# Weight splits behind the exponentials, the keys' low part ahead of the routing, and other orders at the ends of two stages

## What is computed

```python
x = x + tanh(g_xattn[0]) * L0_xattn(layernorm(x), ctx)   # 16 heads of 64, causal, softmax
x = x + tanh(g_ffn[0])   * L0_ffn(layernorm(x))          # 8 experts + 4 zero experts, top 2
x = x + tanh(g_xattn[1]) * L1_xattn(layernorm(x), ctx)   # 16 heads of 8, softmax
x = x + tanh(g_ffn[1])   * L1_ffn(layernorm(x))          # 8 routed experts (top 2) + 2 shared
```

## Time and profile before

| | us |
|---|---|
| median of 3 runs | 267.52 |
| lowest, highest | 266.63, 267.69 |
| the profiled execution | 266.27 |
| its span, first to last instruction | 264.5 |
| busy: PE / DVE / ACT / POOL | 246.9 / 185.1 / 118.8 / 73.9 |
| mean granted clock of TensorE | 0.996 |

### The profile page before, as it was taken

The page is one execution under the profiler, slowest core; times in us unless marked ns, Lnnn a source line. Parts: engine busy times, 40 slices in busy tenths (PEclk is TensorE's granted clock), DMA queues, the critical chain, the costliest instruction groups (busy, mean ns, idle before and its releaser), DMA issues.

```text
span 264.5 us, 7195 instructions
## 1 busy us (share of the span) xinstructions
PE 246.9 (93%) x2917; PEld 207.7 (79%) x2917; DVE 185.1 (70%) x487; ACT 118.8 (45%) x207; POOL 73.9 (28%) x93
## 2 busy tenths in 40 slices
PE   8979999989999999988999999999689999999994
PEld 2557778978899888867999999888566888787783
DVE  1646788866563998899327588446785996887773
ACT  2565455555422455425124344654346767423210
POOL 2356384535531633341001023000210332201100
PEclk9999999999999999999999999999999999999998
DMA  6619600040000000059591000340000000000011
GB/s 192 205 45 267 201 4 4 2 121 1 2 2 0 4 2 2 0 196 297 183 377 38 0 2 0 119 161 1 2 0 2 2 5 2 4 1 2 0 40 40
DMA packets 13232, 16.75 MB, mean 63 GB/s; under 512 B 2064, under 2 KB 10640, under 8 KB 13072
## 3 DMA queue, kind: packets, MB, share of 16 engines
q1 hardware_dynamic: 13056, 16.03, 18.9%
q10 hardware_dynamic: 144, 0.26, 0.5%
HBM read 12.62 MB, written 3.67 MB: 62 GB/s over the span
## 4 chain that ended last, share of the span: by engine, by line
PE 75%; DVE 13%; POOL 4%; issue 4%; ACT 3%; DVEq 0%; POOLq 0%
PE OC L1238 11%; PE MB L1191 5%; PE MB L1081 5%; PE SP L1152 5%; PE OC L1174 5%; PE TP L1161 5%; PE MB L1082 4%; PE MB L1083 4%; PE SP L1088 3%; PE OC L1180 2%; PE SP L1081 2%; PE SP L1083 2%; PE SP L1082 2%; PE MB L1328 2%; PE TP L1376 2%
## 5 line engine op out<-in xcount | busy, mean ns | idle before, releaser
L415 POOL TENSOR_TENSOR S_sb<-S_sb,nmax 128x512 f32<-128x512 f32 x32 | 33.2, 1041 | 38.9 <-DVE nmax L767 38.9
L896 DVE SCALAR_TENSOR_TENSOR x_sb<-OC,gate,x_sb 128x128 f32<-128x128 f32 x64 | 18.0, 344 | 22.4 <-PE OC L1238 22.3
L1238 PEld LDWEIGHTS OC<-f_w,hid 128*128 128x128 f32 x256 | 30.9, 192 | 1.4
L758 DVE TENSOR_TENSOR S_sb<-SP,maskb 128x512 f32<-128x512 f32 x32 | 21.9, 685 | 14.1 <-PE SP L1152 13.9
L1238 PE MATMUL OC<-f_w,hid 128*128 128x128 f32 x256 | 31.4, 276 | 0.0
L767 DVE TENSOR_REDUCE nmax<-S_sb 128x4 f32<-128x512 f32 x32 | 22.0, 686 | 1.1
L539 ACT ACTIVATE PT<-TP 128x512 f32<-128x512 f32 x32 | 19.0, 593 | 7.2 <-PE TP L1161 7.1
L1161 PE MATMUL TP<-id_sb,S_sb 128*128 128x128 f32 x128 | 19.6, 275 | 1.9 <-POOL S_sb L415 1.8
L385 POOL TENSOR_SCALAR var_eps<-mv 128x4 f32<-128x4 f32 x8 | 2.0, 246 | 67.3 <-DVE mv L710 67.3
L523 ACT ACTIVATE arena_f<-MB 128x512 f32<-128x512 f32 x16 | 9.6, 599 | 23.8 <-PE MB L1083 23.3
L1174 PE MATMUL OC<-PT,arena_f 128*32 128x128 f32 x512 | 17.7, 275 | 2.7 <-issue 2.1
(11 more groups left out here) (218 smaller groups left out, 586.4 us busy)
## 6 DMA issues: line engine op xcount, KB each, us to landing
k_dram<-f_r SPq DMA_DIRECT2D x4, 512.0 KB, 9.2
arena_f<-in_zeros SPq DMA_DIRECT2D x1, 2048.0 KB, 9.6
arena_r<-k_dram SPq DMA_DIRECT2D x1, 2048.0 KB, 8.0
w_raw<-in_w SPq DMA_DIRECT2D x4, 384.0 KB, 4.1
ew_raw<-in_f0w SPq DMA_DIRECT2D x1, 1024.0 KB, 7.1
f_w<-in_f0w SPq DMA_DIRECT2D x1, 1024.0 KB, 10.6
arena_r<-q_dram SPq DMA_DIRECT2D x2, 512.0 KB, 4.4
ew_raw<-in_f1w SPq DMA_DIRECT2D x1, 640.0 KB, 10.8
```

What stands on the lines that cost most here:

```text
L415: g.tensor_tensor(S_sb[:, b], S_sb[:, b], nmax[:, b].unsqueeze(2).to_broadcast([P, H4, P]), ALU.add).then_inc(shifted, 1)
L758: v.tensor_tensor(S_sb[:, b].rearrange("p (r a) k -> p r a k", r=2), SP[:, :, 2 * P * b:2 * P * (b + 1)].rearrange("p r (a k) -> p r a k", ...
L896: ins = v.scalar_tensor_tensor(x_sb[:, b, :], OC[:, n % 2, batch(t)], gate0[:, b, e:e + 1], x_sb[:, b, :], ALU.mult, ALU.add)
L1238: ins = mm(OC[:, n % 2, batch(t)], hid[:, n % 2, c, batch(t)], f0_w2[:, e, c, :], start=(c == 0), stop=(c == 1))
```

## The change

- ACT: `split_w0(1,0)` and `split_w0(1,1)` go ahead of the first `queries0`, and in units 0 to 13 `exp0(u,1)` goes ahead of the unit's hooks. POOL: its halves of the splits go one unit later (`split_w0(2,*)` from unit 0 to 1, `split_w0(3,*)` from 2 to 3, `split_f0` from 6..9 to 7..10), `add_bias(0,0)` from 3 to 4 and `best_difference(0,0)` from 14 to 15.
- DVE: part 1 of `route_best(0,0)` goes from unit 14, where it stood ahead of `keys1`, to the head of unit 15's hooks.
- Second attention on PE: `spread_queries(2)` and `(3)` go ahead of `turned1(2,0)`, `maxima1(3)` between the two `turned1(2,*)`, `scores1(4,*)` ahead of `values_of(1)`; at b = 7 `output1(0,0)` goes ahead of `maxima1(7)` (in the ring too), and 3 clock-keeping matmuls stand where there were 5.
- Second expert stage: `spread_gates(4)` goes from turn 4 to turn 3, ahead of `logits(1,1)`; `gates_turn(1)` goes ahead of `hidden1(6)`, and ACT's `gates_hi(1)` from behind turn 6 to behind turn 5. In the last turn DVE makes both products in two halves of 256 tokens, and PE waits for the second half only ahead of its third token block.

```diff
@@ ring_order
-        uses += ([("m", 7), ("y1", 0, 0), ("y1", 0, 1), ("o", 5)] if b == 7 else
+        uses += ([("y1", 0, 0), ("m", 7), ("y1", 0, 1), ("o", 5)] if b == 7 else
...
-        if pair1(n) < C1 - 1:
+        if pair1(n) < C1 - 1 and n != 4:
             uses.append(("b", n))
-        uses += {2: [("t", 3, 1)], 3: [("l", 1, 1)], 5: [("g", 1)]}.get(n, [])
+        uses += {2: [("t", 3, 1)], 3: [("b", 4), ("l", 1, 1)], 5: [("g", 1)]}.get(n, [])
@@ gpsimd
-            hooks = {0: [lambda: split_w0(2, 0), lambda: split_w0(2, 1)],
-                     2: [lambda: rstd_of(0, 1), lambda: split_w0(3, 0), lambda: split_w0(3, 1)],
-                     3: [lambda: add_bias(0, 0)], 5: [lambda: add_bias(0, 1)],
-                     6: [lambda: split_f0(0)], 7: [lambda: split_f0(1)], 8: [lambda: split_f0(2)],
-                     9: [lambda: split_f0(3)], 10: [lambda: rstd_of(1, 0)], 14: [lambda: best_difference(0, 0)]}
+            hooks = {1: [lambda: split_w0(2, 0), lambda: split_w0(2, 1)], 2: [lambda: rstd_of(0, 1)],
+                     3: [lambda: split_w0(3, 0), lambda: split_w0(3, 1)],
+                     4: [lambda: add_bias(0, 0)], 5: [lambda: add_bias(0, 1)],
+                     7: [lambda: split_f0(0)], 8: [lambda: split_f0(1)], 9: [lambda: split_f0(2)],
+                     10: [lambda: rstd_of(1, 0), lambda: split_f0(3)], 15: [lambda: best_difference(0, 0)]}
@@ scalar
             values0(0, 0)
+            split_w0(1, 0)
+            split_w0(1, 1)
             queries0(0, 0)
             queries0(0, 1)
             values0(0, 1)
-            split_w0(1, 0)
-            split_w0(1, 1)
...
                         exp0(u, 0)
                         values0(s, 1)
+                    exp0(u, 1)
                 for hook in hooks.get(u, ()):
                     hook()
                 if s >= STEPS:
                     exp0(u, 0)
-                exp0(u, 1)
+                    exp0(u, 1)
...
-            hooks = {1: [lambda: gates_hi(0)], 3: [...], 6: [lambda: gates_hi(1)]}
+            hooks = {1: [lambda: gates_hi(0)], 3: [...], 5: [lambda: gates_hi(1)]}
@@ vector, hidden1
+                if n == N1 - 1:
+                    wait_full(dve, ("b", n))
+                    for w in range(2):
+                        tok = slice(2 * P * w, 2 * P * (w + 1))
+                        v.tensor_tensor(hid[:, n % 2, 1, tok], hid[:, n % 2, 0, tok], bank[:, 1, tok], ALU.mult).then_inc(up1, 1)
+                        dve.wait_ge(up1, 2 * n + 2 * w + 1)
+                        v.tensor_tensor(hid[:, n % 2, 1, tok], hid[:, n % 2, 1, tok], ring(("b", n))[:, tok], ALU.mult
+                                        ).then_inc(up1, 1)
+                    return
@@ vector, hooks of the first attention
-                     14: [lambda: route_best(0, 0, (1,)), lambda: keys1(0), lambda: keys1(1)],
-                     15: [lambda: values1(0), lambda: values1(1), lambda: route_gates(0, 0)]}
+                     14: [lambda: keys1(0), lambda: keys1(1)],
+                     15: [lambda: route_best(0, 0, (1,)), lambda: values1(0), lambda: values1(1), lambda: route_gates(0, 0)]}
@@ tensor, expert1
+                    if n == N1 - 1 and t == 1:
+                        pe.wait_ge(up1, 2 * N1 + 2)
@@ tensor, second attention
             spread_queries(1)
+            spread_queries(2)
+            spread_queries(3)
             turned1(2, 0)
-            spread_queries(2)
+            maxima1(3)
             turned1(2, 1)
-            spread_queries(3)
             for b in range(3, B):
                 if b == B - 1:
+                    output1(0, 0)
                     maxima1(b)
-                    output1(0, 0)
-                    keep_clock(area_for("t", b, 0)[:, 0, 0:256], 5)
+                    keep_clock(area_for("t", b, 0)[:, 0, 0:256], 3)
                     output1(0, 1)
...
                 if b == 3:
-                    maxima1(b)
-                values_of(b - 2)
-                if b > 3:
-                    maxima1(b)
-                scores1(b + 1, 0)
-                scores1(b + 1, 1)
+                    scores1(b + 1, 0)
+                    scores1(b + 1, 1)
+                    values_of(b - 2)
+                else:
+                    values_of(b - 2)
+                    maxima1(b)
+                    scores1(b + 1, 0)
+                    scores1(b + 1, 1)
@@ tensor, second expert stage
             for n in range(2, N1):
-                if pair1(n) < C1 - 1 and n < N1 - 1:
+                if n == 5:
+                    gates_turn(1)
+                if pair1(n) < C1 - 1 and n not in (4, N1 - 1):
                     spread_gates(n)
                 if n + 1 < N1:
                     hidden1(n + 1)
                 if n == 3:
+                    spread_gates(4)
                     logits(1, 1)
-                if n == 5:
-                    gates_turn(1)
```

More of the change, by code:

```diff
@@ L692, in _ @@
             copy_outputs(B - 1)
-            hooks = {1: [lambda: gates_hi(0)], 3: [lambda: xnT_flat_copy(1), lambda: xnT_hi_copy(3, 1)], 6: [lambda: gates_hi(1)]}
+            hooks = {1: [lambda: gates_hi(0)], 3: [lambda: xnT_flat_copy(1), lambda: xnT_hi_copy(3, 1)], 5: [lambda: gates_hi(1)]}
             for n in range(N1):
```

## The result

| | us |
|---|---|
| changed kernel: median of 5 runs, lowest, highest | 262.56, 262.40, 266.69 |
| kernel before, beside it: median of 5 runs | 267.52 |
| ratio changed / before, 95% interval | 0.984, 0.980 to 0.988 |
| profiled execution of the changed kernel, its span | 266.69, 264.9 |

The change makes the kernel 1.6% faster, 4.2 us by the ratio; 3.3 was forecast for it. Executions of both kernels fall into steps by TensorE's mean granted clock. Changed: 262.2 to 262.8 at 0.999 or more, 264.2 at 0.993 and 266.7 to 267.0 at 0.977 to 0.981. At full clock the medians are 266.3 and 262.5: **3.8 us**.

A forecast was written before the change was run, and what follows sets the result against it. PE's work bounds the kernel, busy 246.9 of 264.5 us, so only waits can be won. Terms 2.2 + 0.55 - 0.4 + 0.8 + 0.15 = 3.3 off median 267.52 give 264.2 us, range 262.4 to 266.2.

The forecast's parts named there:

- Units 0 and 1: First attention's start: waits for POOL's split and for an exponential go, the late shift keeps part; gain 1.0 us.
- Units 2 and 3: Exponential ahead of splits gives 0.5 us, freed shift 0.2; running gain 1.7, then 1.3 at unit 4 after DVE blocking.
- L717 beside POOL's splits: Unit 3: moved splits slow DVE's normalising, 1.10 us lost there; held by the first split alone, running gain 1.3.
- the upper value: Running gain 1.9 us at unit 4 if DVE's L717 loses nothing beside POOL's splits; the lower value was 0.8.
- Units 4 to 7: Late copy costs 0.7 us at unit 5, cancelled by its earlier exponential; units 6 and 7 gain 0.4.
- Unit 12: xnT_hi_copy(1,0) comes 0.9 us later behind the exponential, with no slack before unit 13's transposes: 0.9 lost.
- Units 14 and 15: Routing moved behind unit 15's mask removes PE's waits of 0.65 and 0.66: gain 1.4 us, routing still covered.
- Second attention: b = 3: earlier spread queries gain 0.55 us; b = 7: new ring wait for the residual costs 0.4.
- Rival 3: Longer wait before output1(0,1) at b = 7 lowers the granted clock; kernel slower, 267.9 with 7 us low; chance 0.03.
- Second experts: Earlier gates remove waits at 249.45 and 251.54, leaving 0.5 us idle at gates_turn(1): gain 0.8, bounds 0.3 and 1.1.
- Last turn: DVE products in halves let expert1(9) end about 0.15 us earlier, bounds -0.1 and +0.3.
- rival 4: Whole kernel, more than forecast: no loss at unit 3 and all of b = 3; gain 4.5, 263.0 us; chance 0.15.

The follow-up runs named there:

- e10: Kernel before with only ACT's split_w0(1,0) and (1,1) moved ahead of queries0(0,0): 265.68 us at full clock, ratio to the kernel before 0.995.
- e11: Kernel before with only exp0(u,1) moved ahead of ACT's hooks in units 0 to 13: 266.0 us at full clock, ratio to the kernel before 0.996.
- e5: Kernel before with only route_best(0,0) part 1 and best_difference moved from unit 14 to 15: median 266.08 us, 264.5 at full clock, ratio 0.995.
- e2: Changed kernel with the xnT_hi copies of units 4 and 12 ahead of exp0(u,1) again: median 261.03 us, 260.92 at full clock, ratio to before 0.977.
- e6: Changed kernel with the second attention's b = 3 order of before put back: 262.9 us at full clock, ratio to the kernel before 0.989.
- e4: Changed kernel with b = 7 in PE's and the ring's order of before: 262.07 us at full clock, ratio to the kernel before 0.985.
- e7: Changed kernel with the second experts' gates in the order of before: median 264.87 us, one of 12 at full clock (264.02), ratio to before 0.992.
- e8: Changed kernel with 28 instead of 16 covering matmuls behind turned1(0,1): 262.27 to 269.13 us over six runs, ratio to the kernel before 0.987.
- e1: The changed kernel run again, unaltered: median 263.47 us of 6, 262.5 at full clock, ratio to the kernel before 0.984.
- e3: Changed kernel with POOL's split_f0(3) moved from unit 10 to 11: 262.04 us at full clock, ratio to the kernel before 0.986.
- e12: Changed kernel with 1 instead of 16 covering matmuls behind turned1(0,1): 263.97 to 264.72 us five times and 267.71, ratio to the kernel before 0.990.
- e9: Changed kernel with the edits of e2, e3 and e4 together: median 260.67 us, 260.04 at full clock, ratio to the kernel before 0.975.

## Why the prediction was right, and where it wasn't

The sum was 3.3 and at full clock 3.8 came. It held because most terms did, and because the misses had opposite signs: 0.85 too much at units 2 and 3, some 0.4 at units 4 to 7 and 0.25 at the second experts, against 0.85 lost at unit 11 and 0.2 at the last turn. That they cancelled in part is luck.

**Units 0 and 1: held.** 1.0 forecast, 1.0 measured. e10 shows that ACT's early split alone brings only half of it; the exponential ahead of the hooks alone brings 0.65 at `outputs0(0)` and 0.3 at `outputs0(1)` (e11).

**Units 2 and 3: the gain was mis-sized, 0.7 before blocking, 1.55 measured.** The step that failed is "POOL's splits ... behind `shift(3,1)` they free about 0.2". I read how late the shift was from PE, which came to the transposes at 38.45 with no wait to be seen. POOL's and DVE's own rows of before tell more:

```profile
35.41 1.98 POOL L392 TENSOR_TENSOR arena_r<-w_raw,arena_r 128x512 fp32r<-128x512 f32 x2
37.35 2.04 POOL L415 TENSOR_TENSOR S_sb<-S_sb,nmax 128x512 f32<-128x512 f32 x2
...
35.52 0.69 DVE L767 TENSOR_REDUCE nmax<-S_sb 128x4 f32<-128x512 f32 x1
```

The maximum was there at 36.21 and the shift began at 37.35, 1.14 late. PE didn't wait only because it was late itself, by the 0.51 of the earlier trace rows and a stall of 0.45 with no releaser inside `outputs0(1)`, at 29.67. In e5, whose code is that of before here, the stall doesn't occur, PE is 0.55 earlier at unit 2, waits 0.57 for the shift at unit 3, and is where it was. In e10 and e11 PE comes earlier still and waits 0.89 and 1.15. So without the moved splits the exponential's gain at unit 2 is lost again at unit 3 (e11), and with them units 2 and 3 give 1.55. The splits were not moved alone; that they would give little by themselves is argued from PE's missing wait at 38.45. In the changed kernel the shift follows its maximum directly:

```profile
34.79 1.04 POOL L415 TENSOR_TENSOR S_sb<-S_sb,nmax 128x512 f32<-128x512 f32 x1 [0.23 <-DVE nmax L768]
36.11 1.04 POOL L415 TENSOR_TENSOR S_sb<-S_sb,nmax 128x512 f32<-128x512 f32 x1 [0.28 <-DVE nmax L768]
...
37.61 2.18 DVE L718 SCALAR_TENSOR_TENSOR xn<-x_sb,mv,rstd 128x128 f32<-128x128 f32 x4
```

**L717 beside POOL's splits: the number nearly held, the reading behind it didn't.** The last line is the collision that the prediction priced (L718 now): 2.18 us, against 2.24 beside `add_bias` and 1.14 alone. It cost 0.54 at unit 4, 0.4 forecast. The prediction chose between DVE held by the first split alone and held by both, and took the first. One instruction at a time (the timeline from 37.9 to 38.2 and from 38.6 to 38.9), the trace shows both:

```profile
37.11 1.27 POOL L392 TENSOR_TENSOR arena_r<-w_raw,arena_r 128x512 fp32r<-128x512 f32 x1
37.61 0.92 DVE L718 SCALAR_TENSOR_TENSOR xn<-x_sb,mv,rstd 128x128 f32<-128x128 f32 x1
...
38.34 0.78 POOL L392 TENSOR_TENSOR arena_r<-w_raw,arena_r 128x256 fp32r<-128x256 f32 x1
38.45 0.81 DVE L718 SCALAR_TENSOR_TENSOR xn<-x_sb,mv,rstd 128x128 f32<-128x128 f32 x1
```

Each of the first two of L718 ends 0.15 us behind one of the splits (38.53 and 38.38, 39.26 and 39.12) and takes 0.92 and 0.81; the other two take 0.34. The trace of before, read in the same way:

```profile
38.35 1.05 POOL L415 TENSOR_TENSOR S_sb<-S_sb,nmax 128x512 f32<-128x512 f32 x1
39.11 0.43 DVE L717 SCALAR_TENSOR_TENSOR xn<-x_sb,mv,rstd 128x128 f32<-128x128 f32 x1
39.47 1.36 DVE L717 SCALAR_TENSOR_TENSOR xn<-x_sb,mv,rstd 128x128 f32<-128x128 f32 x1
```

The first ends 0.15 behind the shift L415, the second 0.15 behind L410 (39.35 and 1.33). So the shift held DVE as well, and the prediction's case for the upper value was misread. The Trainium skill (SBUF — State Buffer, Who interferes with whom) has whichever of the two comes second blocked until the other's instruction ends, and all four pairs agree. DVE lost 1.04 us and not the whole 2.0 of the splits because it came to them 0.5 us after the first had begun; that the cost came near the forecast is luck.

**Units 4 to 7: mis-sized, 0.8 for 0.4.** The late copy cost 0.55 (e2), 0.7 forecast, though PE shows only 0.19 of it as a wait. With the copy in its old place, e2 gains 1.36 from unit 4 to 7, which is the exponentials alone, where 0.7 and 0.4 were forecast.

**Unit 11: missed, -0.85.** The sentence that failed is "POOL's halves have no one waiting". I asked who reads the split and not who stands behind it on POOL, which the shift of every unit does. For `split_f0(0)` to `(2)` there was room; `split_f0(3)` shares its unit with a power.

**Unit 12: held.** 0.9 forecast, 0.88 measured, and e2 gives 0.9 back. **Units 14 and 15: held.** 1.4 forecast, 1.45 measured, 1.43 alone by the trace of e5; the routing's cover sufficed.

**Second attention: held.** b = 3 gave 0.52 (0.55 forecast), b = 7 took 0.38 (0.4 forecast), and e6 and e4 reverse each. The wait there is 1.09 us with three matmuls in front.

**Rival 3, the clock at b = 7, did occur in some executions.** In the profiled execution of the changed kernel the clock is 1.00 from 197 to 220 us and 0.50 from 220.5 to 223.5, right behind that wait of 1.10. The profiles of e2, e7 and e8 have the same fall behind the same wait; those of e1, e3, e6 and e12 have the wait and no fall; the six without the wait (before, e4, e5, e9, e10, e11) have none. By an estimate from the windows, 220 to 224 us lost 4 x (1 - 0.57) = 1.7 us; the rest of the 4.2 by which this execution is longer than the 262.5 at full clock lies in the first dip, which was longer here than in e1. Three of the 11 executions of the changed kernel took 266.7 to 267.0, more than the kernel before at full clock; the median isn't one of them. The prediction gave it 0.03, with one execution of before as its reason against. A mean of 0.981 or less stands in 7 of 42 executions of the kernels with this wait and 16 covering matmuls, and in 3 of 105 of those without it. This speaks for the wait as what brings it on, but no run was made to test that, and the kernel before has executions at 0.979 too, none of them profiled.

**Second experts: mis-sized, 1.05 for 0.8**, inside its bounds. PE idles 0.18 at `gates_turn(1)` where 0.5 was forecast (from e3), and not at all at `spread_gates(6)`:

```profile
244.74 0.60 PE L1399 MATMUL MB<-id_sb,gate 128*64 128x128 f32 x4 [0.18 <-DVE gate L881]
```

**Last turn: nothing, -0.07 for +0.15.** From turn 7 to the last `finish` it is 5.45 us before (255.77 to 261.22) and 5.52 in e3 (251.63 to 257.15). The edit puts the wait for the spread gates ahead of the first product, which doesn't read them:

```profile
254.15 0.39 PE L1408 MATMUL MB<-q_hi,ctxT_lo 128*128 128x512 f32 x1
...
254.68 0.42 DVE L977 TENSOR_TENSOR hid<-hid,SP 128x256 f32<-128x256 f32 x1 [1.04 <-PE MB L1408]
```

Before, DVE idled 0.71 us there, behind `hidden1`; now 1.04. By an estimate from these two, the 0.33 us are what the halves would have gained. No run had the wait moved, so this is read from the trace and not tried.

**The median.** The prediction took 3.3 from a baseline median of 267.52, which lies in the step at 0.992; four of the changed kernel's five runs were at full clock. So the time came out 1.6 under the forecast, 0.16 above the range's lower end, with the gain only 0.5 above it. Two sums of the rivals are off as well: 267.9 for rival 3 needs 3.7 us lost, not 7 us of PE's work at the low level, which would lose 7; and rival 4's terms add to 4.25 (0.6 at unit 3 and 0.35 at b = 3), not 4.5.

## What to carry to other kernels

How late a step is must be read on the engine that does it, from its input's end to its own start: an engine that comes late itself shows no wait, and an edit that makes it earlier then gives nothing until the step behind it is moved too. When work moves on a queue, ask first who stands behind it there, and only then who reads it; the losses at units 5, 11 and 13 and at b = 7 were of this kind, the last on the ring's list, and taking them back gave another 2.5 us. Where executions fall into steps by the granted clock, compare within a step, and read every dip of the clock row before ruling one out: the wait made at b = 7 cost 0.4 us in every execution and stood right before a fall worth about 1.7 us in some.

## What the runs showed of the hardware

The granted clock falls to 0.50, the 1.2 GHz level, at the start of the second attention in some executions and not in others of the same kernel. The mean is below full in 4 of 11 executions of the changed one, in all 6 with 15 of the 16 covering matmuls gone, in 4 of 6 with the wait covered; in the profiles it begins at 188 to 193 us, in e8 at 197. A mean of 0.987 with the fall from 188 us (e12) took about 2 us more. At b = 7, behind a wait of 1.09 to 1.10 us, the clock fell in 4 of 8 profiled executions; e8's 6.6 us are for both falls, 10.5 and 7 us long. The wait of 1.56 at 17 us brought none in the profiled execution of before, nor did the 1.55 of e5 and e11.

In every pair read here a DVE instruction with two inputs in SBUF that meets an instruction of POOL that reads SBUF ends 0.15 us behind it: 0.92, 0.81 and 1.36 us for one of L717, 0.34 alone, and 0.92 for one of L913, 0.28 alone (e3: POOL's split ends at 92.76, it at 92.91).

A stall of PE with no releaser can appear in one execution and be absent in the next of the same code (0.45 us at 29.67 of before, not in e5); here it cost nothing, as the shift behind it was late anyway.
